# Long units of TensorE work laid as two halves around the score bursts of a four-layer attention kernel

## The reference

```
x = x + attn_a(layernorm(x))   # squared: (q.k)**2, causal, times v, over its sum; q, k normed per head
x = x + ffn(layernorm(x))      # gated: softmax attention, one key head and one value head per token,
                               #        picked by the largest gate
x = x + attn_b(layernorm(x))   # mqa: softmax attention, one key and value head shared by 16 query heads
x = x + ffn(layernorm(x))      # gated, again
# each: scores = q @ k.T (1024 x 1024 a head, lower triangle), probs = exp or square,
#       out = probs @ v, sums = probs @ 1, out / sums, then (squared, mqa) out @ Wo.T
```

## Time and profile before

| | |
|---|---|
| median of three runs | 4967.37 us (4939.61, 4967.37, 4968.83) |
| profiled execution | 4950.15 us, its span 4948.4 us |
| TensorE (PE) matmul busy | 4254.0 us, 86% |
| DVE, ACT, POOL busy | 1771.8, 1551.4, 850.5 us |
| DMA | 115.65 MB, mean 23 GB/s |
| granted TensorE clock, mean | 0.951 of full |

### The profile page before, as it was taken

How to read it: one execution, slowest core, us unless ns; L and a number is a source line. 1 busy time by engine, 2 the same in 40 slices (tenths; PEclk the granted TensorE clock), 3 DMA queues, 4 the chain that set the end, 5 groups by cost and what they waited for, 6 DMA issues and landing times.

```text
span 4948.4 us, 76270 instructions
## 1 busy us (share of the span) xinstructions
PE 4254.0 (86%) x32674; PEld 1835.6 (37%) x32674; DVE 1771.8 (36%) x2666; ACT 1551.4 (31%) x1985; POOL 850.5 (17%) x1495
## 2 busy tenths in 40 slices
PE   7899999969797887887888888888898987978886
PEld 4444434324333333333333333333333333333332
DVE  1222222224334433344343343433434344333342
ACT  1443343421323223233333333332223233232333
POOL 1212121110102102012021111212012012020011
PEclk9999999989999898999989999999999998999999
DMA  1001010030001001001010010101001001010010
GB/s 60 18 17 36 9 43 5 31 95 8 15 1 39 14 1 52 1 3 50 1 52 1 20 33 7 46 1 52 1 1 52 1 18 35 1 52 1 1 35 27
DMA packets 63404, 115.65 MB, mean 23 GB/s; under 512 B 8672, under 2 KB 9184, under 8 KB 63072
## 3 DMA queue, kind: packets, MB, share of 16 engines
q1 hardware_dynamic: 63072, 110.77, 6.9%
HBM read 77.19 MB, written 33.55 MB: 22 GB/s over the span
## 4 chain that ended last, share of the span: by engine, by line
PE 60%; DVE 6%; ACT 4%; issue 4%; POOL 2%; DMA 2%; SPq 0%; POOLq 0%; DVEq 0%
PE banks L1030 16%; PE banks L989 11%; PE banks L943 9%; PE banks L973 8%; PE banks L937 7%; DVE maxima_soft L771 5%; ACT probs_soft L692 4%; PE banks L970 3%; PE banks L998 2%; PE banks L1127 2%; DMA tiles_soft<-out 1%; POOL rest_soft L665 1%; POOL tiles_soft L597 1%; PE banks L1039 0%; PE banks L949 0%
## 5 line engine op out<-in xcount | busy, mean ns | idle before, releaser
L771 DVE TENSOR_REDUCE maxima_soft<-banks 128x2 f32<-128x1024 f32 (+3 forms) x1152 | 1036.5, 952 | 1507.3 <-PE banks L998 924.8
L692 ACT ACTIVATE probs_soft<-banks 128x1024 f32<-128x1024 f32 (+1 forms) x960 | 848.5, 936 | 1286.4 <-PE banks L973 1286.3
L989 PE MATMUL banks<-k_soft,q_soft 32*128 32x512 f32 (+3 forms) x4608 | 585.1, 578 | 215.9 <-ACT probs_soft L692 215.7
L606 POOL TENSOR_SCALAR_AFFINE_SELECT probs_soft<-probs_soft 128x512 f32<-128x512 f32 x384 | 239.2, 635 | 1841.5 <-ACT probs_soft L692 1839.2
L973 PE MATMUL banks<-q_soft,k_soft 32*128 32x512 f32 (+3 forms) x4608 | 487.2, 504 | 0.0
L1030 PE MATMUL banks<-probs_soft,v_soft 128*32 128x512 f32 (+3 forms) x4608 | 423.7, 510 | 2.0 <-POOL probs_soft L606 2.0
L1030 PE MATMUL banks<-probs_soft,ones 128*32 128x512 f32 (+3 forms) x4608 | 401.4, 489 | 0.0
L970 PE MATMUL banks<-shift_soft,ones 32*128 32x512 bf16 (+3 forms) x2304 | 201.2, 336 | 218.3 <-DVE maxima_soft L771 195.4
L989 PEld LDWEIGHTS banks<-k_soft,q_soft 32*128 32x128 f32 x4608 | 197.2, 194 | 463.5 <-issue 449.3
L692 ACT ACTIVATE probs_squared<-banks 128x1024 f32<-128x1024 f32 (+1 forms) x320 | 282.8, 936 | 239.8 <-PE banks L973 239.5
L1030 PEld LDWEIGHTS banks<-probs_soft,v_soft 128*32 128x32 f32 x4608 | 137.7, 113 | 278.6 <-issue 253.7
(11 more groups left out here) (151 smaller groups left out, 4206.8 us busy)
## 6 DMA issues: line engine op xcount, KB each, us to landing
tiles_soft<-out SPq DMA_DIRECT2D x96, 256.0 KB, 2.8
rest_soft<-out SPq DMA_DIRECT2D x96, 256.0 KB, 3.2
out<-rest_soft SPq DMA_DIRECT2D x96, 256.0 KB, 2.0
tiles_squared<-in_x SPq DMA_DIRECT2D x32, 256.0 KB, 2.9
rest_squared<-in_x SPq DMA_DIRECT2D x32, 256.0 KB, 3.2
out<-rest_squared SPq DMA_DIRECT2D x32, 256.0 KB, 2.0
raw_wq<-in_squared_wq SPq DMA_DIRECT2D x1, 1024.0 KB, 6.0
raw_wk<-in_squared_wk SPq DMA_DIRECT2D x1, 1024.0 KB, 8.2
```

The lines of the kernel that those rows point to most:

```text
L606: ins = pool.affine_select(out=cells, in_=cells, compare_op=ALU.is_ge, fill=0.0, base=0, pattern=[[0, HG], [1, P]], channel_multiplier=-1)
L692: act.activation(slot(ph, n)[:, 2 * a:2 * a + 2, 0:width], score_pair(e, a)[:, :, 0:width], ACT.Exp if soft else ACT.Square, scale=SCALE). ...
L771: ins = dve.reduce_max(m["maxima"][:, ph % 2, 2 * a:2 * a + 2, t, p], score_pair(e, a)[:, :, col:col + P * blocks], AX_X)
L989: ins = pe.matmul(psum[:, score_bank(e, i), col:col + P * blocks], m["q"][D * i:D * i + D, ph % NG, P * t:P * t + P], k_of(ph)[D * i:D * i ...
```

## The change

The list of events gets a new kind, `("more", event)`: the first half of a long unit. The event itself then issues the rest. Halves are by the number of matmuls: 8 and 8 of `av` and `sm` (so 512 and 384 columns in the first half of A and C, 256 and 128 in the second), 2 and 2 of a projection. `phase` puts the two halves of `av` and then of `sm` at four neighbouring half steps (C from 1, A from 8, B from 14), and `spread` takes halves as separate pieces, with new weights. `two_banks` then goes over the list: a unit may be open (begun and not ended) while at most one other unit passes, since there are two work banks; if a further one would start, the open one is ended first. Units are numbered, and so given their bank, by where they end. The other engines see no change but the order: they read a unit when it is complete. `mxt` of the second half of the rows moves ahead of the first rows burst. No matmul is added or taken away.

```diff
--- before.py
+++ after.py
@@ -60,12 +60,14 @@
 NRB = len(ROW_BURSTS)
 HALVES = 2 * NKB
 
-VALUES_AT = {"C": 3, "A": 9, "B": 15}
-
-
-WEIGHT = {"keys": 0.9, "rows": 0.7, "av": 1.5, "sm": 1.5, "q": 1.8, "q2": 1.8, "k2": 1.8, "kvar": 0.9, "v2": 1.9,
...
+VALUES_AT = {"C": 1, "A": 8, "B": 14}
+
+
+WEIGHT = {"keys": 1.3, "rows": 1.2, "av": 3.2, "sm": 3.2, "q": 3.5, "q2": 3.5, "k2": 3.5, "kvar": 0.9, "v2": 3.5,
...
+
+HALVED = ("av", "sm", "q", "q2", "k2", "v2", "ks", "kall", "vall")
 
 UNITS = ("av", "sm", "q", "q2", "k2", "kvar", "v2", "ln", "gt", "gtt", "kall", "vall", "kt", "ks", "vs", "vst",
          "mxt", "rs", "rw", "out")
@@ -110,10 +112,21 @@
     return first, queries[1]
 
 
+def halved(event, kinds):
+    return event[0] in HALVED or event[0] == "out" and kinds[event[1]] != "gated"
+
+
+def in_halves(events, kinds):
+    return [e for event in events for e in ([("more", event)] if halved(event, kinds) else []) + [event]]
+
+
 def weight(event, kinds):
+    if event[0] == "more":
+        return weight(event[1], kinds)
+    share = 0.5 if halved(event, kinds) else 1.0
     if event[0] == "out":
-        return 0.5 if kinds[event[1]] == "gated" else 1.8
-    return WEIGHT.get(event[0], 0.0)
+        return share * (0.9 if kinds[event[1]] == "gated" else 3.5)
+    return share * WEIGHT.get(event[0], 0.0)
 
 
 def sums_done(kind, ph, c):
@@ -135,7 +148,7 @@
         if more and k < NRB:
             at[2 * k + 1].append(("rows", ph + 1, k))
     if kinds[s] != "squared":
-        at[1].append(("mxt", ph, 1))
+        at[1].insert(0, ("mxt", ph, 1))
     if more:
         at[5].append(("mxr", ph + 1, 0))
         at[8].append(("mxt", ph + 1, 0))
@@ -148,18 +161,20 @@
         if of < 0:
             continue
         h = VALUES_AT[part]
-        at[h].append(("av", of, part))
-        at[h + 1].append(("sm", of, part))
+        at[h].append(("more", ("av", of, part)))
+        at[h + 1].append(("av", of, part))
+        at[h + 2].append(("more", ("sm", of, part)))
+        at[h + 3].append(("sm", of, part))
         if part != "B":
             for event, later in sums_done(kinds[of // NG], of, 0 if part == "A" else 1):
-                at[h + 1 + later].append(event)
+                at[h + 3 + later].append(event)
     return at
 
 
 def spread(kinds, halves, work):
 
     fixed = [sum(weight(e, kinds) for e in h) for h in halves]
-    queue = [(e, since, until) for part, since, until in work for e in part]
+    queue = [(e, since, until) for part, since, until in work for e in in_halves(part, kinds)]
     events, carry = [], 0.0
     for n, h in enumerate(halves):
         events += h
@@ -174,6 +189,31 @@
             events.append(queue.pop(0)[0])
         carry = max(room, 0.0) if queue else 0.0
     return events + [e for e, _, _ in queue]
+
+
+def two_banks(events):
+
+    placed, ended, since = [], set(), {}
+
+    def end(e):
+        since.pop(e, None)
+        ended.add(e)
+        placed.append(e)
+        for other in since:
+            since[other] += 1
+
+    for e in events:
+        starts = e[0] == "more" or e[0] in UNITS and e not in since and e not in ended
+        while starts and since and (len(since) == 2 or since[next(iter(since))]):
+            end(next(iter(since)))
+        if e[0] == "more":
+            since[e[1]] = 0
+            placed.append(e)
+        elif e[0] not in UNITS:
+            placed.append(e)
+        elif e not in ended:
+            end(e)
+    return placed
 
 
 def plan(kinds):
@@ -217,7 +257,7 @@
     events += [("rload", stages - 1, t) for t in range(TILES)]
     for t in range(NT):
         events += [("out", stages - 1, t)] + [("rload", stages - 1, t + TILES)] * (t + TILES < NT)
-    return events
+    return two_banks(events)
 
 
 class Count:
@@ -910,14 +950,24 @@
         @block.tensor
         def _(pe):
             known = set()
+            begun = set()
+
+            def share(terms, e, opening):
+
+                terms = list(enumerate(terms))
+                if opening:
+                    begun.add(e)
+                    return terms[:len(terms) // 2]
+                return terms[len(terms) // 2:] if e in begun else terms
 
             def free(e):
-                if unit[e] >= 2:
+                if unit[e] >= 2 and e not in begun:
                     pe.wait_ge(sg.work_free[bank(e)], unit[e] // 2)
                 return work[:, bank(e), :]
 
             def ready(e, ins):
-                ins.then_inc(sg.work_ready[bank(e)], 1)
+                if not opening:
+                    ins.then_inc(sg.work_ready[bank(e)], 1)
 
             def need(e):
 
@@ -932,14 +982,16 @@
                         old = bursts[(use - 3) // 2]
                         pe.wait_ge(sg.probs_ready if old[0] == "keys" else sg.maxima_ready, 2 * of_kind[old] + (use - 3) % 2 + 1)
 
-            def channel_product(out, s, c, wt, cols):
-                for kc in range(KC):
+            def channel_product(e, c, wt, cols):
+                out = free(e)
+                for kc, _ in share(range(KC), e, opening):
                     ins = pe.matmul(out, wt[:, kc, cols], m["xnT"][:, kc, CHUNK * c:CHUNK * c + CHUNK],
                                     start=(kc == 0), stop=(kc == KC - 1))
                 return ins
 
-            def token_product(out, t, wt, cols):
-                for kc in range(KC):
+            def token_product(e, t, wt, cols):
+                out = free(e)
+                for kc, _ in share(range(KC), e, opening):
                     ins = pe.matmul(out, m["xnT"][:, kc, P * t:P * t + P], wt[:, kc, cols], start=(kc == 0), stop=(kc == KC - 1))
                 return ins
 
@@ -950,7 +1002,9 @@
                                     start=True, stop=True)
                 return ins
 
-            for e in events:
+            for event in events:
+                opening = event[0] == "more"
+                e = event[1] if opening else event
                 u = e[0]
                 if u == "keys":
                     _, ph, n = e
@@ -1004,6 +1058,7 @@
                     s, g = divmod(ph, NG)
                     numbers, products = parts_of(part)
                     out = free(e)
+                    fresh = e not in begun
                     pe.wait_ge(sg.probs_ready, 2 * (of_kind["keys", ph, numbers[-1]] + 1))
                     if part != "B":
                         pe.wait_ge(sg.probs_masked, masks_until(ph, part))
@@ -1015,11 +1070,11 @@
                     if not soft:
                         pe.wait_ge(sg.values_scaled, ph + 1)
                         c = "ABB".index(part) if part != "C" else 1
-                        if u == "sm" and part != "C":
+                        if u == "sm" and part != "C" and fresh:
                             pe.wait_ge(sg.query_squares, place["qsq", ph, c] + 1)
                             pe.matmul(out, k["head_eps"][:].rearrange("p i d -> p (i d)"), m["query_square"][:, c],
                                       start=True, stop=True)
-                    for x, (kb, q0, width, n, col) in enumerate(products):
+                    for x, (kb, q0, width, n, col) in share(products, e, opening):
                         for i in range(HG):
                             if u == "sm":
                                 left = k["ones"][:] if soft else m["key_weight"][:, ph % NG, kb, i:i + 1].broadcast_to([P, D])
@@ -1043,12 +1098,12 @@
                     s, g = divmod(ph, NG)
                     for t in range(TPC * c, TPC * c + TPC):
                         need(("ln", s, t))
-                    ready(e, channel_product(free(e), s, c, w_of(s)["wk" if u == "k2" else "wq"], slice(P * g, P * g + P)))
+                    ready(e, channel_product(e, c, w_of(s)["wk" if u == "k2" else "wq"], slice(P * g, P * g + P)))
                 elif u == "ks":
                     _, s, c = e
                     for t in range(TPC * c, TPC * c + TPC):
                         need(("ln", s, t))
-                    ready(e, channel_product(free(e), s, c, w_of(s)["wk"], slice(0, P)))
+                    ready(e, channel_product(e, c, w_of(s)["wk"], slice(0, P)))
                 elif u in ("gt", "vs"):
                     _, s, c = e
                     for t in range(TPC * c, TPC * c + TPC):
@@ -1064,13 +1119,15 @@
                 elif u in ("kall", "vall"):
                     _, s, t = e
                     need(("ln", s, t))
-                    ready(e, token_product(free(e), t, w_of(s)["wk" if u == "kall" else "wv"], slice(0, C)))
+                    ready(e, token_product(e, t, w_of(s)["wk" if u == "kall" else "wv"], slice(0, C)))
                 elif u == "v2":
                     _, s, pair, n = e
                     out = free(e)
-                    for x in range(2):
-                        need(("ln", s, 2 * n + x))
-                        ins = token_product(out[:, 2 * P * x:2 * P * x + 2 * P], 2 * n + x, w_of(s)["wv"], slice(2 * P * pair, 2 * P * pair + 2 * P))
```

(16 more changed lines are left out.)

## The result

The changed kernel takes 4804.32 us (median of four runs, 4795.98 to 4810.55), the kernel before on the same chip 4953.49. The ratio is 0.970 (95% interval 0.965 to 0.975): 3.0% faster, where 2.5% was forecast.

The account below looks back on a forecast made before the run. PE's own stream was taken to bound the kernel. 4950 - 239 + 83 + 98 - 60 gave 4832 us for the profiled execution, and the forecast was 4845 us, with an 8 in 10 range of 4725 to 4935.

Parts of the forecast that it names:

- Term 1: PE ahead of score bursts: work in more gaps covers waits, which fall from 449 to 210 us, a gain of 239.
- Term 2: PE between separated halves: more changes between kinds of work, 0.14 or 0.20 us each, cost 83 us more.
- the upper bound: Term 2 with the way back from burst to unit charged too: 185 us instead of 83; chance 0.08.
- Term 3: PE at openings of units: waits for a work bank still being read cost 98 us more, bounds 47 and 246.
- Term 4: PE's clock: of some 150 us lost at half clock, 40% comes back as waits shrink, 60 us less.
- What I put at nothing: DVE, ACT and POOL work, mxt ahead of the first rows burst, and SP's loads and stores: no effect on the time.
- the new weights merely move the lumps: Rival on the order of PE's work: no real gain, time near 4950 us; chance 0.03.
- The slower rival: The two work banks become the bound: 246 us of waits instead of 98 and more, 5203 us; chance 0.05.

Follow-up runs that it names:

- e1: The change with only av and sm laid as halves, projections whole: 4719.57 us, 0.955 of before.
- e2: The change with only projections and their like laid as halves, av and sm whole at their old places: 4994.48 us, 1.010 of before.
- e3: The change with products of parts A and C reordered so that both halves have 640 columns: 4749.32 us, 0.961 of before.
- e4: The change, but a unit takes, when it begins, the work bank whose last unit ended longest ago: 4684.28 us, 0.948 of before.
- e9: Projections alone in halves (e2) with the free choice of bank of e4: 4871.30 us, 0.987 of before.
- e8: The change with the mxt transposes put back behind the first rows burst: 4808.97 us, 0.972 of before.
- e5: The kernel before with the new weights alone, no halves and no other places: 4985.61 us, 1.007 of before.
- e6: The change with both the balanced halves of e3 and the free bank of e4: 4638.81 us, 0.938 of before.
- e11: e6 with the weights of the kernel before: 4602.11 us, 0.932 of before.
- e10: e2 (projections alone in halves) with the weights of the kernel before: 4971.47 us, 1.006 of before.

## Why the prediction was right, step by step

The span moved by -140 us. In the measured columns: bursts -259, work +74, units +98, clock -35, layer norm -17. The terms were -239, +83, +98, -60, and none, in sum -118.

**Term 1, right in mechanism and nearly in size.** The rule (base less the work in the gap) was read from the earlier trace rows, and the order's count of empty gaps gave the rest. e1 and e2 test it by changing how many halves there are, and the burst waits came near the forecasts (244 for 255 to 265, 359 for 350 to 365). e3 tests it by changing only their length: a half of 1.28 us against a base of 1.4 us after a rows burst leaves 0.1 us, and 0.15 was measured, though the forecast of the total was wrong, as said there. The short gaps were mis-sized: I took the second halves at 0.3 x 2.29 = 0.69 us; a half that is followed by a wait takes 0.86 (2159.40 above), so 0.28 us of wait remained ahead of rows bursts and 0.60 ahead of key bursts, not 0.65 at both (and 192 x 0.65 is 125, not 127).

**Term 2, right in its sum, not in where the price falls.** The halves of `av` B take 1.85 and 1.86 us (2171.52 to 2173.37, 2174.44 to 2176.30), together 3.71 against 3.57: 0.14. Half a projection ahead of a burst takes 1.92 us (2072.96 to 2074.88), twice that is 3.84 against 3.63: 0.21. The work grew by 74 us, forecast 83. But I read the 0.20 us of a projection as the price of the way from unit to burst alone and took the way back at nothing. PE in the kernel before, a whole projection behind a transpose:

```profile
2080.75 3.60 PE L943 MATMUL banks<-g_wv,xnT_soft 128*128 128x512 f32 x8
2084.28 0.39 PE L970 MATMUL banks<-shift_soft,ones 32*128 32x512 bf16 x4
```

It takes 3.53 us, where one among its like takes 3.43 and one with a burst at each end 3.63: about 0.10 us at either end. The halves in e4 say the same: 1.91 us behind a key burst (2015.14 to 2017.05), 1.81 behind transposes (2018.62 to 2020.43). The length of the burst, which I had looked at, does not show the way back; the length of the unit behind it does. A separated half has both ends, so the sum came out; beside a transpose it costs less, which may be why work in e2 grew by 18 us where 35 were forecast (in e1 by 49, forecast 44). So a projection pays at both ends, about 0.10 us each; the 185 us of the upper bound charged the way back a second time.

**Term 3, the direct size right, its reach missed.** The 98 us are in the units' column. What failed is the sentence that took the clock by the sum of all waits: e4 removes 81 us of these waits and gains 120, e9 removes 49 and gains 123. A wait of 2 us for a bank can cost PE more than its own length, since the clock may fall behind it. PE in the changed kernel:

```profile
2142.80 3.57 PE L995 MATMUL banks<-g_wv,xnT_soft 128*128 128x512 f32 x4 [2.34 <-DVE inverse_soft L917]
2146.31 0.45 PE L1024 MATMUL banks<-shift_soft,ones 32*128 32x512 bf16 x4
...
2150.48 1.71 PE L1085 MATMUL banks<-probs_soft,v_soft 128*32 128x512 f32 x16 [0.76 <-ACT shift_soft L718]
```

The mean clock from 2142.80 to 2146.31 is 0.54, and half a projection takes 3.51 us instead of 1.92. Behind the like wait of 2.37 us (2072.96) the clock stayed full (1.00 from 2072.96 to 2076.00), so not every one does it. As I priced it, the change's own bank trouble was 98 us; by e4 it is 107 to 120.

**Term 4, mis-sized: -35 us for -60.** Half clock fell from 489 to 374 us, by 24%, where burst waits had fallen by 58%. The 40% of the prediction were a choice: the waits that it names, 449 to 308, fall by 31%. The 150 us that it took as lost before were too few: of the 489 us PE was idle in 125, and half of the rest is 182. The new bank waits gave part of the gain back: with the free bank (e4) half clock is 315. Falls stand behind short waits too: in the changed kernel the mean clock was 1.00 from 2147 to 2163 and 0.53 from 2163.4 to 2165.4, behind waits of 0.76, 0.58, 0.62 and 1.26 us, and the burst at 2163.39 took 2.01 us, not 1.14.

**What I put at nothing.** `mxt` was indeed covered (e8). The rival "the new weights merely move the lumps", to which I gave 0.03, held a grain: the weights cost 0.7% by themselves (e5), and taking them back in the best version brought 0.7% (0.938 to 0.932, e6 and e11). I had looked at the weights only together with the halves. The upper bound of term 2, with both ways charged in full, to which I gave 0.08, was right about the ways and wrong about the price, as said there. The slower rival, the two work banks as the bound, did not decide for the whole change but does for half of it: with projections alone in halves the kernel is slower than before until the banks are chosen freely.

**Open.** e10 is slower than before by 0.6%, while in its profiled execution the idle time is 21 us less: the work is 22 us more, and the rest, some 41 us, is the clock (598 us at half, in the slowest of four executions). That bank waits cause this is shown by e9 with the new weights, not with the old. Layer norm's 17 us came with the other order, and no run here isolates them.

## What to carry to other kernels

Where an engine waits in many small equal pieces, read the base wait once (1.26 us here), count in the order how much work stands in each gap, and cut the work so that no piece is much shorter than the base: here equal pieces beat equal counts by 55 us (e3). A piece that is held open pins its buffer, so choose the buffer when the piece begins, not when it ends, or its opening waits behind a reader's queue (2.37 us at the second place, gone in e4). And test the parts of a change apart even where the whole is faster: here one part was a loss of some 75 to 85 us inside a gain of 150.

## What the runs showed of the hardware

The time at half clock does not follow the idle time. Ahead of bursts and units PE is idle for 455 us in e2 and for 491 in the kernel before, and is at half clock for 610 us in e2 and 489 before. Taking 49 us of bank waits out of e2 (e9) took 161 us off its time at half clock; adding 20 us of burst waits by the weights (e5) added 73, or 40 by the medians of the runs. Behind unit waits of 1.5 us and more the clock was at half within 2 us in 21 of 26 cases in e2, but in 4 of 8 in e9 and 3 of 10 in e4; it also fell behind a run of shorter ones (0.76, 0.58, 0.62 and 1.26 us, to a mean of 0.53 over the next 2 us, in the change), and what in the placing of the waits decides it, these runs do not say.

A projection between two bursts, which are four matmuls side by side, takes 3.63 us, 3.53 with a transpose ahead of it and 3.43 among its like: about 0.10 us at each end. A cut of `av` or `sm` costs 0.14 us for both ends together; how that divides was not read.
